# Two graph layers on one core: order of the first loads, first projection, and attention turn rearranged

## The reference, cut to what matters

```python
# layer 0
h = relu(einsum('ts,bsh->bth', adj, x @ Wg0 + bg0))
h = relu(einsum('ts,bsh->bth', adj, h @ Wg1 + bg1))
for p in range(1, 5):                      # LSTM over windows of p nodes
    wins = h[:, :nw * p, :].reshape(Bv * nw, p, Hd)
    last = _lstm_last(Wih[p - 1], Whh[p - 1], bih[p - 1], bhh[p - 1], wins)
    h = h.at[:, idx, :].set(last)          # last node of each window
x = layernorm(x + h)
# layer 1: graph attention over 256 edges, 4 heads
Xq, Xv = H @ W_lin.T, H @ W_val.T
e = (leaky_relu(Xq[:, src] + Xq[:, dst]) * a).sum(-1) + log(A0[src, dst] + EPS)
attn = softmax of e over the edges of one source
Y = segment_sum(attn * Xv[:, dst], src) @ W_out.T
x = layernorm(x + Y)
```

## Time and profile before

| | us |
|---|---|
| median of 3 runs | 916.77 (914.58 to 917.51) |
| profiled execution, its own time | 916.78 |
| its span in the trace | 915.0 |
| PE busy, share of the span | 876.2 (96%) |
| DVE busy | 694.7 (76%) |
| ACT busy | 612.2 (67%) |
| POOL busy | 175.0 (19%) |
| mean granted TensorE clock | 0.995 |

### The profile page before, as it was taken

One profiled execution on the slowest core, in us unless ns is written; L12 is line 12 of the kernel. 1 busy time (PEld: TensorE's weight loads), 2 busy tenths in 40 slices (PEclk: granted clock), 3 DMA queues, 4 the chain that ended last, 5 costly groups with the idle time before them and its releaser, 6 DMA issues.

```text
span 915.0 us, 15431 instructions
## 1 busy us (share of the span) xinstructions
PE 876.2 (96%) x5411; PEld 761.5 (83%) x5411; DVE 694.7 (76%) x1560; ACT 612.2 (67%) x1116; POOL 175.0 (19%) x509
## 2 busy tenths in 40 slices
PE   6999999999999999999999999999998999999795
PEld 6888888877787779999998887877787888887684
DVE  4777777777778787778777777676787887886885
ACT  1777777777777666676676666666786677775344
POOL 0000000000000000000000010012564455655665
PEclk9999999999999999999999999999999999999998
DMA  4211221001000000000000177775360011111122
GB/s 108 73 47 58 70 59 47 24 1 47 1 1 0 1 1 1 1 1 1 1 1 1 29 156 162 161 183 139 81 151 1 25 36 31 29 37 47 36 70 70
DMA packets 43260, 45.44 MB, mean 50 GB/s; under 512 B 2576, under 2 KB 40112, under 8 KB 40112
## 3 DMA queue, kind: packets, MB, share of 16 engines
q1 hardware_dynamic: 39504, 27.47, 10.5%
q0 software_dynamic: 2304, 16.78, 9.0%
q10 hardware_dynamic: 1376, 0.22, 0.1%
HBM read 19.29 MB, written 8.39 MB: 30 GB/s over the span
## 4 chain that ended last, share of the span: by engine, by line
PE 76%; DVE 8%; DMA 6%; issue 5%; ACT 2%; POOL 1%; ACTq 0%; DVEq 0%; POOLq 0%
PE psum L443 7%; PE psum L444 7%; PE psum L445 7%; PE psum L1135 6%; PE psum L1062 6%; PE psum L461 5%; PE psum L457 5%; PE psum L458 5%; DMA hT_lo<-x_stage 3%; PE psum L361 3%; PE psum L379 3%; PE psum L389 3%; PE psum L1146 2%; PE psum L1118 2%; PE psum L352 2%
## 5 line engine op out<-in xcount | busy, mean ns | idle before, releaser
L561 ACT ACTIVATE work<-psum,bias 128x512 f32<-128x512 f32 (+1 forms) x408 | 233.3, 623 | 29.2 <-PE psum L461 28.6
L443 PE MATMUL psum<-hT_hi,w_hi 128*128 128x512 f32 (+1 forms) x408 | 148.7, 365 | 3.3 <-ACT work L561 2.6
L444 PE MATMUL psum<-hT_lo,w_hi 128*128 128x512 f32 (+1 forms) x408 | 147.4, 361 | 0.0
L445 PE MATMUL psum<-hT_hi,w_lo 128*128 128x512 f32 (+1 forms) x408 | 147.2, 361 | 0.0
L545 ACT ACTIVATE work<-work 128x512 f32<-128x512 f32 (+1 forms) x112 | 63.8, 570 | 104.4 <-DVE work L813 73.1
L973 POOL DMA_DIRECT2D hT_lo<-hT_hi x8 | 7.3, 918 | 558.5 <-DVE hT_lo L788 539.3
L820 DVE TENSOR_TENSOR work<-work 128x512 f32<-128x512 f32 (+1 forms) x112 | 68.5, 612 | 54.1 <-ACT work L545 54.1
L457 PE MATMUL psum<-hs_hi,w_hi 128*128 128x512 f32 (+1 forms) x288 | 103.8, 360 | 0.8 <-DVE hs_hi L786 0.7
L461 PE MATMUL psum<-hs_lo,w_hi 128*128 128x512 f32 (+1 forms) x288 | 104.4, 362 | 0.0
L458 PE MATMUL psum<-hs_hi,w_lo 128*128 128x512 f32 (+1 forms) x288 | 103.1, 358 | 0.0
L443 PEld LDWEIGHTS psum<-hT_hi,w_hi 128*128 128x128 f32 x408 | 76.8, 188 | 17.5 <-ACT work L561 5.4
(11 more groups left out here) (191 smaller groups left out, 1856.4 us busy)
## 6 DMA issues: line engine op xcount, KB each, us to landing
work<-x SPq DMA_DIRECT2D x32, 256.0 KB, 3.0
x_stage<-x_by_feature SPq DMA_DIRECT2D x8, 1024.0 KB, 5.2
hT_lo<-hT_hi POOLq DMA_DIRECT2D x8, 1024.0 KB, 9.2
hT_lo<-x_stage POOLq DMA_DIRECT2D x8, 1024.0 KB, 7.0
out<-x_kept SPq DMA_DIRECT2D x32, 256.0 KB, 2.3
work<-L_gnn_Wih SPq DMA_DIRECT2D x4, 256.0 KB, 3.0
work<-L_gnn_Whh SPq DMA_DIRECT2D x3, 256.0 KB, 3.0
bg_all<-L_gnn_bg ACTq DMA_DIRECT2D x2, 64.0 KB, 5.6
```

Of the source, the lines that this page charges most:

```text
L443: pe.matmul(out, w_hi[:, w, g, :], xh, start=True, stop=False)
L444: pe.matmul(out, w_hi[:, w, g, :], xl, start=False, stop=False)
L445: mm = pe.matmul(out, w_lo[:, w, g, :], xh, start=False, stop=(t == 0))
L561: op = act.activation(gate[s][g][:, 0:ph.width], psum[:, 4 * s + g, 0:ph.width], ACT.Tanh if g == G else ACT.Sigmoid, bias=bias[:, b:b + 1])
```

## The change

1. **Loads.** `adj` moves from the head of SP's queue to the head of ACT's; `Wg0` moves to ACT; the edge columns (`edge_col_i`, 4-byte elements) and the attention vector `a` move from ACT to SP. SP's order is now x0, x1, edge rows, edge columns, x2, LSTM piece 0, the three layer 1 weights, `a`. ACT's is adj, bg0, Wg0, then a one-column activation (which brings its table load with it), then the column of bg0, Wg1, bg1, bih, bhh.
2. **Start on TensorE.** Five matmuls of ones stand ahead of the transposition of `adj` and one behind it (`run_warm`). Slot 0 comes ahead of `degrees`, and each one-time step up to `log_to_rows` moves one slot later, on PE, ACT and DVE alike (`rank_rows` from behind slot 0 to behind slot 1, and so on). DVE copies `adjT` before it negates bg0, and makes `rank_rows` after slot 1. The logarithm on ACT moves from slot 4 to slot 5, between sigmoids, which adds one table load.
3. **First LSTM item of window 2.** Its gates I and G from the input are issued in front slot 36, ahead of the last O gate of window 1 (`first_input`), into banks AX and AH.
4. **First values.** `values(0)` stands behind `queries(0)` in the last LSTM item; ACT's `value_hi(0)` stands ahead of that item's gates and DVE's `value_lo(0)` ahead of its cell.
5. **Attention.** In back slots 13, 21 and 29 PE makes queries and values first and `attention_by_edge` behind them. DVE keeps `attention_out` where it was. In slot 37 there are no queries, so nothing moves.

The diff, cut to its core:

```diff
@@ front, run_sync
-        sp.dma_start(adj_sb[:, :], adj).then_inc(S["adj_loaded"], 16)
         load_x(0)
-        sp.dma_start(wg0[:, :], Wg0).then_inc(S["wg0_loaded"], 16)
+        load_x(1)
         sp.dma_start(edge_row_i[:, :], ...)
-        load_x(1)
+        for j, e in enumerate((src, dst)):
+            sp.dma_start(edge_col_i[:, j, :], ...).then_inc(S["cols_loaded"], 16)
+        load_x(2)
         load_piece(0)
...
-        load_x(2)
+        sp.wait_ge(S["a_zero"], 1)
+        for h in range(HEADS):
+            sp.dma_start(T.a_wide[...], a[h]...).then_inc(S["a_loaded"], 16)
@@ front, run_tensor
+        def first_input(g, bank, free):
+            ph = phases[1]
+            pe.wait_ge(free, tiles)
+            pe.wait_ge(S["tiles_done"], ph.batches // BT + CREDIT)
...
+            pe.matmul(out, w_hi[:, w, g, :], xh, start=True, stop=False)
+            pe.matmul(out, w_hi[:, w, g, :], xl, start=False, stop=False)
+            pe.matmul(out, w_lo[:, w, g, :], xh, start=False, stop=True).then_inc(gate_psum[g], 1)
@@ slot(n), ahead of gate_product(O, n - 5)
+            if n - 5 == tiles - 1:
+                first_input(I, AX, S["axT_ready"])
+                first_input(G, AH, S["ahT_ready"])
@@
+        def run_warm(count):
+            for _ in range(count):
+                pe.matmul(psum[:, GATE_BANK[O], 0:P], ones[:, :], ones[:, :], start=True, stop=True)
+
+        pe.wait_ge(S["consts"], 1)
+        run_warm(5)
         pe.wait_ge(S["adj_loaded"], 16)
         pe.wait_ge(S["ident_ready"], 1)
         pe.transpose(psum[:, SIDE, 0:P], adj_sb[:, :], ident[:, :]).then_inc(S["adjT_psum"], 1)
-        degrees()
+        run_warm(1)
+        pe.wait_ge(S["adjT_ready"], 1)
         for n in range(SLOTS):
             slot(n)
             if n == 0:
+                degrees()
+            elif n == 1:
                 rank_rows()
...
-                    for g in ((I, G, O) if t == 0 else (F, I, G, O)):
+                    first = ph is phases[1] and it == 0 and k == 0
+                    for g in ((O,) if first else (I, G, O) if t == 0 else (F, I, G, O)):
@@ front, run_scalar
+        act.dma_start(adj_sb[:, :], adj).then_inc(S["adj_loaded"], 16)
         act.dma_start(bg0_all[:, :], ...)
-        for j, e in enumerate((src, dst)):
-            act.dma_start(edge_col_i[:, j, :], ...)
+        act.dma_start(wg0[:, :], Wg0).then_inc(S["wg0_loaded"], 16)
+
+        act.wait_ge(S["consts"], 1)
+        act.activation(first_act[:, :], ones[:, 0:1], ACT.Copy)
...
-            if n == 4:
+            if n == 5:
                 act.wait_ge(S["eps_done"], 1)
                 act.activation(log_adj[:, :], adj_edge[:, :], ACT.Ln)...
...
+                    if is_last(ph, it, k):
+                        entry.value_hi(act)
@@ back, slot(n) on PE
-            if n > 0 and n % GT == LAG % GT and has(n - LAG):
-                attention_by_edge((n - LAG) // GT)
             if has(n):
                 if n:
                     queries(n)
-                values(n)
+                    values(n)
+            if n > 0 and n % GT == LAG % GT and has(n - LAG):
+                attention_by_edge((n - LAG) // GT)
@@ back, enter_query
         queries(0)
+        values(0)
@@ back, vector
+        def first_projections():
+            scaled_query(0)
+            value_lo(0)
```

More of the change, by code:

```diff
@@ L26 @@
 Part = namedtuple("Part", "S CREDIT phases sync gpsimd tensor scalar vector")
-Entry = namedtuple("Entry", "turn turned query read order stats scale_query")
+Entry = namedtuple("Entry", "turn turned query read order value_hi stats scale_query")
 class LstmPhase:
@@ L353, in gate_product @@
             pe.matmul(out, w_lo[:, 0, g, :], hT_hi[:, cols], start=False, stop=True).then_inc(gate_psum[g], 1)
+        def first_input(g, bank, free):
+            assert bank == g
+            ph = phases[1]
+            pe.wait_ge(free, tiles)
+            pe.wait_ge(S["tiles_done"], ph.batches // BT + CREDIT)
+            xh, xl = windows_at(ph, hi_bt, 0, 0, 0), windows_at(ph, lo_bt, 0, 0, 0)
+            w, out = piece_of[1, 0], psum[:, bank, 0:ph.width]
+            pe.wait_ge(S["w_lo_ready"], len(pieces))
+            pe.matmul(out, w_hi[:, w, g, :], xh, start=True, stop=False)
+            pe.matmul(out, w_hi[:, w, g, :], xl, start=False, stop=False)
+            pe.matmul(out, w_lo[:, w, g, :], xh, start=False, stop=True).then_inc(gate_psum[g], 1)
         def slot(n):
@@ L484, in run_scalar @@
         act.dma_start(b_raw[:, 1, :], bhh.rearrange("s (g h) -> (s g) h", g=GATES)).then_inc(S["b_loaded"], 16)
-        act.wait_ge(S["a_zero"], 1)
-        for h in range(HEADS):
-            act.dma_start(T.a_wide[h * DH:(h + 1) * DH, T.a_col + h:T.a_col + h + 1], a[h].rearrange("(d o) -> d o", o=1),
-                          allow_slow_non_contiguous=True).then_inc(S["a_loaded"], 16)
         def cut_piece(i):
@@ L758, in run_vector @@
             if n == 1:
+                rank_rows()
+            elif n == 2:
                 sorted_edges()
-            elif n == 2:
+            elif n == 3:
                 ends_and_sames()
@@ L763, in run_vector @@
                 centre_back_weights()
-            elif n == 3:
+            elif n == 4:
                 caps()
                 back_weights()
-            elif n == 5:
+            elif n == 6:
                 log_diagonals()
-            elif n == 6:
+            elif n == 7:
                 log_rows()
@@ L1171, in slot @@
                 output(n - 1 - LAG)
-        return turn, queries, slot
+        return turn, queries, values, slot
     def enter_turn(pe, k):
-        turn, _, _ = tensor_steps(pe)
+        turn, _, _, _ = tensor_steps(pe)
         turn(k)
@@ L1182, in enter_query @@
     def enter_query(pe):
-        _, queries, _ = tensor_steps(pe)
+        _, queries, values, _ = tensor_steps(pe)
         pe.wait_ge(FS["wT_ready"], 2)
         queries(0)
+        values(0)
     def run_tensor(pe):
-        _, _, slot = tensor_steps(pe)
+        _, _, _, slot = tensor_steps(pe)
         for name, count in (("ends_ready", 1), ("onehots", 1), ("a_loaded", 16 * HEADS)):
@@ L1194, in enter_read, with enter_value_hi @@
     def enter_read(act, k):
-        read_turned, _, _ = scalar_steps(act)
+        read_turned, _, _, _ = scalar_steps(act)
         read_turned(k)
     def enter_order(act, k):
-        _, order, _ = scalar_steps(act)
+        _, order, _, _ = scalar_steps(act)
         order(k)
+    def enter_value_hi(act):
+        _, _, value_hi, _ = scalar_steps(act)
+        value_hi(0)
     def scalar_steps(act):
@@ L1252, in slot @@
                     query_hi(n)
-                value_hi(n)
+                if n:
+                    value_hi(n)
             g, part = softmax_at(n)
@@ L1267, in slot @@
                 leaky_relu(n, 1)
-        return read_turned, order, slot
+        return read_turned, order, value_hi, slot
     def run_scalar(act):
-        _, _, slot = scalar_steps(act)
+        _, _, _, slot = scalar_steps(act)
         for n in range(LAST):
@@ L1396, in slot @@
                 softmax(g, step)
-        return stats_in, scaled_query, slot
+        return stats_in, first_projections, slot
     def enter_stats(dve, k):
@@ L1404, in enter_scale_query @@
     def enter_scale_query(dve):
-        _, scaled_query, _ = vector_steps(dve)
-        scaled_query(0)
+        _, first_projections, _ = vector_steps(dve)
+        first_projections()
     def run_vector(dve):
@@ L1413, in run_vector @@
             slot(n)
-    entry = Entry(enter_turn, enter_turned, enter_query, enter_read, enter_order, enter_stats, enter_scale_query)
+    entry = Entry(enter_turn, enter_turned, enter_query, enter_read, enter_order, enter_value_hi, enter_stats, enter_scale_query)
     return Part(S, 0, None, run_sync, run_gpsimd, run_tensor, run_scalar, run_vector), entry
```

20 lines of the change are left out of this document (11 added, 9 removed).

## The result

| us | before | after |
|---|---|---|
| median (lowest to highest), 10 runs each | 916.46 (914.58 to 918.50) | 919.38 (915.46 to 921.12) |
| profiled execution, its span | 916.78, 915.0 | 921.12, 919.3 |
| mean granted TensorE clock of that execution | 0.995 | 0.985 |

The ratio of the two is 1.0036, 95% interval 1.0025 to 1.0047: slower by more than a measurement is uncertain, where 911.7 had been forecast. The changed kernel's ten executions spread over 5.7 us, and time follows the granted clock: 915.46 at 0.992, 918.27 at 0.989, 921.12 at 0.985.

The account below looks back on a forecast made before the run. PE, busy 96% of the span, was taken as the bound, so only its gaps or low clock could yield gain. Start 2.5, window boundary 0, entry 1.1 and attention 1.5 made 5.1 off 916.78: 911.7, range 909.5 to 915.2.

Parts of the forecast that it names:

- The start gains 2.5: Start: second bias product at 28.0 instead of 30.89, less 0.4 for three transpositions; bounds 0.3 to 3.7.
- bias + 8.9: Start: sorted rows are read 8.9 us behind the bias landing, taken as 10.9, so at 19.8.
- the forecast's 2.9: Start: second bias product 2.9 us earlier, at 28.0 instead of 30.89, before 0.4 for the transpositions.
- rival 1: Start gives nothing: bias lands at 13.1, start gains 0.3, total 913.9; chance 0.14.
- Rival 2: Start at the low clock after a bias at 13.1: start loses 3.4, total 917.6; chance 0.05.
- b + 3.6 + 0.7: Start, DVE's chain to the sorted rows: bias landing b, permutations 3.6, then max of tile 0, 0.7.
- Window 1 to window 2: gain 0, it costs nothing either: Window boundary: PE only waits longer for the last O gate; O product 0.4 later, its reader 2 us behind.
- Entry: gain 1.1, I take the high clock: Entry of the back: tile 1's gather at 644.45 instead of 645.54, at the high clock; bounds -1.7 to +1.2.
- my lower bound: Entry of the back: if the clock falls all the same, a loss of up to 1.7.
- Attention 1.5: Back slots 13, 21 and 29: gains of 1.1, 0.2 and 0.2; bounds 0 to 1.8.
- Rival 4: Slots 21 and 29: DVE idles 1.2 in each, loss 2.4 instead of gain 0.4, total 914.5; chance 0.05.
- Rival 3: Front slots 5 and 6: ACT's logarithm and table loads hold up PE by 2.8, total 914.5; chance 0.03.

Follow-up runs that it names:

- e13: The kernel before with dummy matmuls in its gaps at the start (5), the entry (12) and back slot 10 (8): 914.04 us, ratio 0.9980.
- e15: The kernel of e11 measured again, beside e13 and e14: 911.75 us, ratio 0.9951 to the kernel before.
- e9: The changed kernel as it is, unfilled, timed again on another chip: 917.27 us, ratio 1.0024 to the kernel before.
- e11: The changed kernel with dummy matmuls at start, entry and slot 10, and the early gates back in their old place: 911.84 us, ratio 0.9956.
- e10: The kernel before with dummy matmuls ahead of the rank rows (5), first values (12) and back slot 11's gather (3): 914.07 us, ratio 0.9979.
- e2: The kernel before with item 3, the early gates of window 2's first item, alone: 916.72 us, ratio 1.0014.
- e3: The kernel before with item 4, the first tile's values in the last LSTM item, alone: 916.19 us, ratio 1.0007.
- e4: The kernel before with item 5, the attention turn behind the projections, alone: 914.58 us, ratio 0.9992.
- e14: e13 with the attention turn behind the projections and no other edit: 912.40 us, ratio 0.9960 to the kernel before.
- e5: The changed kernel with dummy matmuls in all four gaps (start, window boundary, entry, slot 10): 912.84 us, ratio 0.9964 to the kernel before.
- e6: The changed kernel with the 8 dummy matmuls of the start alone: 914.88 us, ratio 0.9987 to the kernel before.
- e1: The kernel before with items 1 and 2 (loads and start) alone, without the early gates: 917.54 us, ratio 1.0021.
- e7: The changed kernel with the 7 dummy matmuls between windows 1 and 2 alone: 915.48 us, ratio 0.9993 to the kernel before.
- e8: The changed kernel with dummy matmuls in back slots 1 (entry) and 10 alone: 914.39 us, ratio 0.9983 to the kernel before.
- e12: e8 again, beside e9 on one chip: 915.54 us, ratio 0.9993 to the kernel before.

## Why the prediction was wrong, step by step

The same five places in six profiled executions, from their timelines. Slot 13's start is the turn's start less its wait in the kernels with the old order of attention.

| us | before | e13 | e15 | after | e9 | e11 |
|---|---|---|---|---|---|---|
| PE's 0.4 wait for ACT near the end of window 1 | 203.69 | 201.66 | 201.15 | 203.63 | 201.32 | 201.33 |
| first queries | 631.40 | 629.18 | 628.86 | 632.92 | 630.62 | 629.08 |
| projections of tile 2 | 646.61 | 642.90 | 642.59 | 648.13 | 644.80 | 642.79 |
| slot 13 starts | 693.04 | 690.04 | 689.63 | 699.00 | 694.73 | 689.74 |
| from there to the end | 221.96 | 221.96 | 220.27 | 220.3 | 220.27 | 220.26 |

- **"The start gains 2.5": the step that failed first.** Its length of the new list was right: bias + 8.9 for the sorted rows (e15: 11.17 + 8.9 = 20.07, measured 20.08) and 8.2 from there to the bias product (7.93). What was wrong is what it was subtracted from. The profiled execution of before had run its start at the low clock (x8 of 2.08 and 1.92 where e13 and e10 have 1.16 and 1.06), and its bias had landed late. I took its 30.89 as the kernel's own.

| us | old start | new start |
|---|---|---|
| b_sum starts | 11.87 in before, 11.02 to 11.49 in e2, e3, e4, e10, e13, e14 | 11.11 to 11.64 in ten profiles |
| from there to the bias product, high clock | 17.56 (e10, e13, e14) | 16.85 (e5, e6, e9, e11, e15) |
| the same, low clock in part | 19.02 in before, 17.66 to 18.34 in e2, e3, e4 | 18.5 to 19.82 (after, e1, e7, e8, e12) |

- So the forecast's 2.9 were 1.0 from a bias that the new order of loads does not bring earlier, and 1.9 from 19.02 less 17.1, where 17.56 less 16.85 gives 0.7. Less the 0.4 of the three transpositions, the start is worth 0.3 at equal bias. The first row of the table of places says 0.5 between e13 and e15, and 0.1 between e10 (201.40) and e11. This is the outcome of rival 1, the start gives nothing, though its bias transfer was not late.
- **Rival 2, the low clock at the start**, had been given 0.05. It came, and by one of the two gaps that it names, the one ahead of tile 1's product, but without the late bias (13.1) that it asks for: at b = 11.11 PE stood still for 2.68 until DVE's max of tile 0. The sum has this max in its chain (b + 3.6 + 0.7) and then prices the products behind it at 0.9 each, as if PE had not stood still. They took 2.05 and 1.91. The bias product stood at 30.54 and not at 33.9, mostly since the bias was 2.0 earlier than in the rival and the sort lost 0.9 (2.78 against 1.89) and not 1.9. In the changed kernel's profile it costs 2.3 (203.63 against 201.33). In e9 PE was late ahead of that place, its wait was 1.60, and the clock behind it 1.00; it costs nothing there.
- **"Window 1 to window 2: gain 0, it costs nothing either"**: the gain was 0, the cost not. Between the first two rows of the table of places the changed kernel takes 429.29 and e9 429.30, e11 427.75: 1.5, from one gap of 1.95 where there had been 1.00 and 0.70. It costs this only when the clock falls: e8 and e12, where it fell too, take 429.24 and 429.27, but e2 and e6 with the same unfilled gap and a granted clock of 1.00 in 210 to 215 take 427.73 and 427.59. I had seen that PE only waits longer there, and did not ask what the clock makes of it. e6's row:

```profile
209.27 0.50 PE L477 MATMUL psum<-hT_hi,w_hi 128*128 128x512 f32 x1 [1.94 <-ACT work L533]
```

- **"Entry: gain 1.1, I take the high clock".** The wait for the values went as forecast, and DVE's piece kept its length: 9.84 from the start of `xq_hi` of tile 0 to the end of tile 1's split queries (636.37 to 646.21), 9.84 before. But the 1.1 was the low clock of before's own profiled entry (0.72 in the earlier trace rows). From `xq_hi` to tile 2's projections the old list takes 10.93 in e13 when the clock holds (642.90 less 631.97), the new one 10.95 in e15. Gain 0, and in the changed kernel the two gaps of 1.51 and 1.95 dropped the clock, as my lower bound had allowed for: 11.76.
- **What I didn't see: slot 10.** When POOL is held up by its transfers, PE waits there for DVE and DVE for POOL. In the eight profiles that have this wait unfilled, PE's is 0.11 or 0.12 shorter than DVE's, from 1.10 (e2) to 2.23 (e9), with the old start and entry (e2, e4, e10) as with the new. So the change did not make the wait. But a fall can follow it, and in the changed kernel's profiles it did. Slots 2 to 13 take 50.87 there, 49.93 in e9 and 46.95 in e11, which fills the gap and whose POOL was on time. In e14, filled too, DVE waited 2.07 for POOL and the clock held: 47.57. So some 0.6 of the changed kernel's 3.9 is POOL's delay, and the rest comes with the low clock, slot 2's included (3.62 for its x16). Why POOL's transfers are late in one execution and not in another, no run shows.
- **"Attention 1.5"** was right: 221.96 to 220.3, 1.7, and 1.64 between e13 and e14. Of it slot 13 gives 1.11: from its start to the value gather on DVE's second product it took 6.80 before (699.84 less 693.04) and 5.69 in e15 (695.32). The other 0.6 lies behind it, where slots 21 and 29 had been forecast at 0.4. Rival 4 is out.
- **Rival 3**, ACT holding PE in slots 5 and 6, is out: in e15 PE has no wait over 0.4 in the stretch from 30 to 48, with loads at 31.23, 35.77 and 38.26. The logarithm follows its load at 37.06, 1.29 after 35.77, so the drain of the Trainium skill (ScalarE: Activation LUTs, What ACT_TABLE_LOAD costs) does not show here either.

The balance of the changed kernel's profiled span against e11's 910.0: start 2.30, boundary 1.54, entry 1.50, slots 2 to 13 3.92, and nothing behind, 9.3 in all, which is 919.3. In medians on one chip the clock and the early gates cost the changed kernel 5.4 (917.27 less 911.84), and the clock costs the kernel before 2.0 (916.00 less 914.04). Less the edits' 2.3 that makes the changed kernel 1.1 slower; measured were 1.5 there and 2.9 in the first comparison. Against the forecast this is two errors: 3.6 of gain for start and entry where 0.65 is there, and, outside rival 2 and the entry's lower bound, nothing for what the clock loses behind the waits.

Open: what the early gates cost beside the clock. At the boundary they cost nothing while it holds (427.72 in e5, filled, and e2 and e6 above, against 427.71 in e15). Yet e5, which has them, is 1.0 slower than e11 and e15, and e2 rose by 1.1 without a fall there in its trace. No run compared them on one chip with all gaps filled, and the intervals of the ratios of e5, e11 and e15 overlap. In e5's profiled execution the 1.0 lies in the wait for POOL's factors: `xq_hi` starts 3.79 behind the first queries, and 2.62 in e11. This distance moves on its own: 2.33 to 3.19 in the profiles without the early gates, 2.63 to 3.79 in those with them.

## What to carry to other kernels

When PE is 96% busy, read the granted clock and the durations of equal matmuls at every place that the sum touches, and take "before" from a stretch at the high clock; a gain measured against a slow stretch can be the clock's and not the edit's. One profile is one execution: the start of before read 1.4 to 1.9 us later than in the three other unfilled profiles of the same list. An edit that joins two short gaps, or moves a wait in front of full work, is priced with the clock's fall behind it. Dummy matmuls in the few real gaps are the cheapest test of this and here were worth more than the change: 2.0 us for the kernel before, 5.4 together with the early gates undone for the changed one.
